# A graph-attention layer with fast matrix multiplication on one Trainium2 core: one block row of V moved ahead of P6, half of the next pair's V ahead of the first output, W's loads ahead of two of x's

## The chip, the cores and the metric

The kernel runs on one core of a Trainium2 chip. TensorE (PE in the profile) multiplies, with its weight loads shown apart as PEld; VectorE (DVE), ScalarE (ACT) and GpSimd (POOL) do the elementwise work; SyncE (SP) issues nearly all DMAs. The metric is the device time of one execution in microseconds, lower is better. Each engine takes its instructions strictly in the order in which they were written, and waits at the head of its queue for semaphores.

## What is computed

```python
output = einsum('bni,io->bno', x, w)          # V, 32 items of 256 x 512
q = einsum('bni,io->bno', x, wq)
k = einsum('bni,io->bno', x, wk)
alpha = einsum('bno,bmo->bnm', q, k)          # 256 x 256 scores of an item
alpha = maximum(alpha, 0) * (adj != 0)
alpha = softmax(alpha, axis=1)
x = layernorm(x + einsum('bnm,bmo->bno', alpha, output))   # fp32, over the last axis
```

## The kernel before

The 32 items of x go in 16 pairs. Slot 0 of the buffers belongs to the even item of work and slot 1 to the odd one: "pair 0" and "pair 1" below are the first two pairs. First G = wq·wkᵀ is formed once (`fill_g`), so that scores are (x·G)·xᵀ. T = x·G and V = x·W are then computed by a Strassen-like scheme: x is four blocks A11, A12, A21, A22, sums of them are S1 to S4, sums of G's and W's blocks are T1, T2, T3 and D4, and seven products P1, P7, P6, P5, P2, P3, P4 (each in two halves) replace eight.

Every fp32 operand X is split: `X_hi` is X cast to fp32r by ScalarE, `X_lo` is X - X_hi, computed by VectorE or GpSimd. A product is three matmuls (`add_chunk`, lines 339 to 341): hi·hi, hi·lo, lo·hi. So each product waits for splits that two other engines deliver in their own written order.

T is computed for two pairs at once (`fill_first_t`, `fill_t`), V by pair (`fill_v`, 14 halves of 6 matmuls). Only pair 0's V is computed plainly, one block row at a time: `fill_first_v(r)` for r = 0 to 3, 12 matmuls of 512 columns each. PE's order before the loop is: G; rows 0, 1, 2 of pair 0's V; `fill_first_t`; the scores of pair 0 (`fill_first_s`, 2 x 24 matmuls of 256 columns); row 3 of pair 0's V; the scores of pair 1 (`fill_s_b(0)`); the output of pair 0 (`fill_first_o`); the V of pair 1 (`fill_v(1, 1, first=True)`). Then a loop over the other groups of two pairs follows, and `fill_last_o`.

Around the scores VectorE does this, in this order: split of T's block A21 of pair 0; `mask(0, 0)` when the first 24 score matmuls are done, two row maxima; split of T's block A11 of pair 1; `mask(0, 1)`, which needs the second 24 score matmuls; split of T's block A12 of pair 1; two row maxima; splits of A22 and A21 of pair 1. `fill_scores(0, 1)` waits for pair 0's fourth T split. `fill_s_b(0)` waits for pair 1's second T split (A12) and `mask(0, 0)`, its second half for the fourth (A21) and `mask(0, 1)`.

SP issues, in order: Wq and Wk by quarters, pair 0's x (`xt`, four blocks), W (four quarters, into `xn`), pair 1's x (into `soft` and `parts`), then later pairs behind waits. GpSimd forms the sums S3, S1, S2, S4 of both pairs, splits some of them, forms T1, T3, T2, D4 of W and splits those.

## Time and profile before

| | us |
|---|---|
| median of 3 runs | 520.92 (520.74 to 521.06) |
| the profiled execution | 520.78 |
| its span in the trace | 519.0 |
| PE busy in the span | 510.6 (98%) |

The span is what the profiler saw of the program; 1.8 us lie around it. In the rows below times count from the span's start. A row of the timeline gives start, duration, engine, line, operation, output<-inputs, and, in brackets, how long the engine sat idle before it and what released it. PE's matmuls overlap, so their pace is read from the distance between starts and not from the durations. The trace shows tiles by name only: W's raw data lie in `xn`, pair 1's sums in `parts` and `adj`.

### The profile page before, as it was taken

What the parts mean: (1) busy time and instruction counts of PE and PEld (TensorE: products, weight loads), DVE (VectorE), ACT (ScalarE), POOL (GpSimd) and SP (SyncE); (2) the same over time, 40 slices, a digit from 0 to 9 for tenths busy, and PEclk for the clock granted to TensorE, in tenths of its full rate; (3) what the DMA queues carried; (4) which work ended last, traced back from release to release, by engine and by line L of the source; (5) the groups of instructions that cost most, each with busy time, mean ns of one, the idle gap of its engine ahead of it and who ended that gap; (6) DMA issues with size and microseconds to landing.
All of it is one profiled execution on the core that took longest, in us unless ns stands there. A gap on an engine that the chain in (4) does not pass through costs nothing.

```text
span 519.0 us, 9822 instructions
## 1 busy us (share of the span) xinstructions
PE 510.6 (98%) x3206; PEld 464.0 (89%) x3206; DVE 379.1 (73%) x744; ACT 330.9 (64%) x756; POOL 263.4 (51%) x199
## 2 busy tenths in 40 slices
PE   8999999999999999999999999999999999999995
PEld 7779998899989998899988999889998999889994
DVE  6997855776848677586866778577684866757586
ACT  6855756386763857649474586638676385764677
POOL 1799884339535377145651486433953537610011
PEclk9999999999999999999999999999999999999998
DMA  8412151044520626025350342405342061501426
GB/s 291 175 61 83 67 182 58 20 124 163 178 84 20 221 62 242 20 61 182 116 203 20 125 139 110 175 20 151 132 179 84 20 222 61 202 1 35 168 90 235
DMA packets 30367, 62.05 MB, mean 120 GB/s; under 512 B 2064, under 2 KB 2320, under 8 KB 30352
## 3 DMA queue, kind: packets, MB, share of 16 engines
q1 hardware_dynamic: 30064, 61.48, 34.7%
q10 hardware_dynamic: 288, 0.39, 0.2%
q8 instruction: 7, 0.11, 0.1%
q14 instruction: 8, 0.07, 0.0%
HBM read 45.09 MB, written 16.78 MB: 119 GB/s over the span
## 4 chain that ended last, share of the span: by engine, by line
PE 95%; DMA 1%; SPq 1%; DVE 1%; issue 1%; ACT 0%; POOLq 0%; POOL 0%; DVEq 0%; ACTq 0%
PE o_bank L339 12%; PE o_bank L340 12%; PE o_bank L341 12%; PE chain L339 11%; PE chain L341 11%; PE chain L340 11%; PE bank_y L339 6%; PE bank_y L340 6%; PE bank_y L341 6%; PE bank_z L341 3%; PE bank_z L340 3%; PE bank_z L339 3%; DMA xn<-in_w 1%; SPq L293 0%; SPq L289 0%
## 5 line engine op out<-in xcount | busy, mean ns | idle before, releaser
L1560 POOL TENSOR_TENSOR s_lo<-xs,s_hi 128x512 fp32r<-128x512 f32 x56 | 76.4, 1378 | 36.7 <-ACT s_hi L727 36.7
L1555 POOL TENSOR_TENSOR a_lo<-xt,a_hi 128x512 fp32r<-128x512 f32 x42 | 57.5, 1375 | 61.3 <-ACT a_hi L719 61.3
L339 PE MATMUL o_bank<-t_hi,a_hi 128*128 128x256 f32 x256 | 72.5, 283 | 0.0
L340 PE MATMUL o_bank<-t_lo,a_hi 128*128 128x256 f32 x256 | 72.4, 283 | 0.0
L341 PE MATMUL o_bank<-t_hi,a_lo 128*128 128x256 f32 x256 | 72.4, 283 | 0.0
L1565 POOL TENSOR_TENSOR rstd<-var_eps,minus_half 128x4 f32<-128x4 f32 x14 | 14.2, 1017 | 92.6 <-DVE var_eps L1202 92.6
L750 ACT COPY parts<-chain 128x256 f32<-128x256 f32 x90 | 33.2, 369 | 43.3 <-PE chain L341 42.1
L1122 DVE TENSOR_TENSOR parts<-parts,bank_y 128x512 f32<-128x512 f32 x32 | 22.0, 688 | 41.9 <-ACT parts L736 25.8
L1551 POOL TENSOR_TENSOR xs<-xt 128x512 f32<-128x512 f32 x28 | 36.8, 1325 | 27.9 <-DMA xt<-in_x_t 27.9
L339 PE MATMUL chain<-w_hi,s_hi 128*128 128x256 f32 x180 | 50.9, 283 | 0.0
L340 PE MATMUL chain<-w_lo,s_hi 128*128 128x256 f32 x180 | 50.9, 283 | 0.0
L341 PE MATMUL chain<-w_hi,s_lo 128*128 128x256 f32 x180 | 50.9, 283 | 0.0
L1188 DVE SCALAR_TENSOR_TENSOR xn<-o_bank,xn 128x512 f32<-128x512 f32 x62 | 42.4, 684 | 10.2 <-PE o_bank L341 10.1
L339 PEld LDWEIGHTS o_bank<-t_hi,a_hi 128*128 128x128 f32 x256 | 49.1, 192 | 0.4
L340 PEld LDWEIGHTS o_bank<-t_lo,a_hi 128*128 128x128 f32 x256 | 49.1, 192 | 0.4
L341 PEld LDWEIGHTS o_bank<-t_hi,a_lo 128*128 128x128 f32 x256 | 49.1, 192 | 0.0
L339 PE MATMUL o_bank<-v_hi,p_hi 128*128 128x512 f32 (+1 forms) x126 | 49.0, 389 | 0.1
L340 PE MATMUL o_bank<-v_lo,p_hi 128*128 128x512 f32 (+1 forms) x126 | 48.9, 388 | 0.0
L341 PE MATMUL o_bank<-v_hi,p_lo 128*128 128x512 f32 (+1 forms) x126 | 48.8, 387 | 0.0
L1110 DVE TENSOR_TENSOR v_lo<-parts,v_hi 128x512 fp32r<-128x512 f32 x45 | 46.8, 1052 | 0.1
L1208 DVE TENSOR_SCALAR xn<-xn,neg_mean,rstd 128x512 f32<-128x512 f32 x56 | 39.3, 723 | 10.1 <-POOL rstd L1565 10.1
L778 ACT CAST t_hi<-parts 128x512 fp32r<-128x512 f32 x24 | 14.8, 621 | 49.8 <-PE o_bank L341 49.8
(209 smaller groups left out, 1648.6 us busy)
## 6 DMA issues: line engine op xcount, KB each, us to landing
xn<-in_x SPq DMA_DIRECT2D x16, 1024.0 KB, 5.2
xt<-in_x_t SPq DMA_DIRECT2D x60, 256.0 KB, 3.1
out<-xn SPq DMA_DIRECT2D x14, 1024.0 KB, 5.3
adj<-in_adj_t SPq DMA_DIRECT2D x16, 512.0 KB, 4.8
xn<-in_wq_t SPq DMA_DIRECT2D x4, 256.0 KB, 4.0
xn<-in_w SPq DMA_DIRECT2D x4, 256.0 KB, 6.9
out<-xn SPq DMA_DIRECT2D x2, 512.0 KB, 3.1
parts<-in_wk_t SPq DMA_DIRECT2D x3, 256.0 KB, 4.5
```

Source lines behind the costliest of these rows:

```text
L339: nc.tensor.matmul(dst, a[0], b[0], start=first, stop=False, skip_group_check=shared)
L340: nc.tensor.matmul(dst, a[0], b[1], start=False, stop=False, skip_group_check=shared)
L341: return nc.tensor.matmul(dst, a[1], b[0], start=False, stop=last, skip_group_check=shared)
L750: nc.scalar.copy(parts[:, PART[product], c, 0], chain_v[:, c]).then_inc(v_copied, 1)
L778: nc.scalar.copy(t_hi[:, u], whole).then_inc(t_hi_ready, 1)
L1110: return nc.vector.tensor_tensor(dst, whole, hi.bitcast(F32), ALU.subtract)
L1122: nc.vector.tensor_tensor(part, part, bank, ALU.add).then_inc(t_summed, 1)
L1188: nc.vector.scalar_tensor_tensor(out=xn[:, slot, r], in0=row.rearrange("q j n -> q (j n)"), scalar=1.0, in1=xn[:, slot, r], op0=ALU.mult, ...
L1208: nc.vector.tensor_scalar(xn[:, slot, r], xn[:, slot, r], neg_mean[:, r:r + 1], rstd[:, r:r + 1], ALU.add, ALU.mult).then_inc(normed, 1)
L1551: nc.gpsimd.tensor_tensor(xs[:, s], a, b, op).then_inc(x_summed[slot], 1)
L1555: nc.gpsimd.tensor_tensor(a_lo[:, slot, u], xt[:, u], a_hi[:, slot, u].bitcast(F32), ALU.subtract).then_inc(a_lo_ready[slot], 1)
L1560: nc.gpsimd.tensor_tensor(s_lo[:, slot, s], xs[:, s], s_hi[:, slot, s].bitcast(F32), ALU.subtract).then_inc(s_lo_ready[slot], 1)
```

## The change

It has four parts.

1. PE: `fill_first_v(3)` moves from behind `fill_first_s` to between P7 and P6 in `fill_first_t`. It writes `o_bank[2]` now, and waits for `g_lo_ready` 3 and the first D4 half. ScalarE's and VectorE's `split_first_v(3)` move forward with it.
2. PE: the first six of the fourteen halves of pair 1's V (`open_v`) come before `fill_first_o`, the other eight (`close_v`) after it. ScalarE's copies of P1 and P6 of pair 1 move ahead of some casts and of pair 1's four exponents.
3. SP, ScalarE, VectorE: W is loaded and split between x's blocks A12 and A21. GpSimd waits for all of pair 0's x to be split before it forms the first sum.
4. Pair 0's S2 is split by GpSimd and not by VectorE. Semaphore targets follow.

```diff
-FIRST_LO = {S3: 1, S2: 2}, {S1: 1, S4: 2}
+FIRST_LO_DVE = {S3: 1}, {S3: 1, S2: 2}
+FIRST_LO_POOL = {S2: 1, S1: 2, S4: 3}, {S1: 1, S4: 2}
...
-        v0_bank = [bank_y[:, 0], o_bank[0][:], o_bank[1][:], o_bank[0][:]]
+        v0_bank = [bank_y[:, 0], o_bank[0][:], o_bank[1][:], o_bank[2][:]]
...
+            load_x0(A11)
+            load_x0(A12)
             for k in range(K):
                 sp.dma_start(w_raw[:, k], w_rows[:, k]).then_inc(w_loaded[k], 16)
+            load_x0(A21)
+            load_x0(A22)
...
                 pe.wait_ge(gt_summed, 8)
                 t_half(P7, 1, both)
+
+                fill_first_v(3)
                 pe.wait_ge(t_copied, 1)
...
                 if r == 3:
 
-                    pe.wait_ge(t_summed, 2)
+                    pe.wait_ge(g_lo_ready, 3)
+                    pe.wait_ge(gt_summed, G_SUMMED[D4, 0])
...
                 fill_scores(0, 0)
+
+                pe.wait_ge(v_lo_ready, 4)
                 pe.wait_ge(t_lo_ready, 4)
                 fill_scores(0, 1)
...
             fill_first_s()
-            fill_first_v(3)
             fill_s_b(0)
+
+            pe.wait_ge(wt_lo_ready, W_ORDER.index(D4))
+            open_v(1, 1)
             fill_first_o()
-            fill_v(1, 1, first=True)
+            close_v(1, 1, first=True)
...
-            exponent(1, 0)
-            exponent(1, 1)
-            copy_v(1, P1, 0)
-            exponent(1, 2)
-            copy_v(1, P1, 1)
-            exponent(1, 3)
             copy_v(1, P6, 0)
             copy_v(1, P6, 1)
+            for r in range(R):
+                exponent(1, r)
...
-            pool.wait_ge(qk_lo_ready, 2 * K)
+            pool.wait_ge(a_lo_ready[0], 4)
             sum_first_x(0, S3)
-
-            pool.wait_ge(w_lo_ready, K)
             sum_first_x(0, S1)
...
             sum_first_x(1, S2)
+            split_first_s(0, S2)
             split_first_s(0, S1)
```

PE's queue where P7 ends and P6 begins, before. `bank_y<-s` is P7, `chain<-s` is P6:

```order
L341 MATMUL bank_y<-s_hi,g_lo 128x512
L339 MATMUL chain<-s_hi,g_hi 128x512
L340 MATMUL chain<-s_lo,g_hi 128x512
L341 MATMUL chain<-s_hi,g_lo 128x512
...
```

PE's queue at the same place in the changed kernel (its `add_chunk` has lines 350 to 352); `o_bank2<-w` is row 3 of pair 0's V, four such groups of three:

```order
L352 MATMUL bank_y<-s_hi,g_lo 128x512
L350 MATMUL o_bank2<-w_hi,a_hi 128x512
L351 MATMUL o_bank2<-w_lo,a_hi 128x512
L352 MATMUL o_bank2<-w_hi,a_lo 128x512
...
L350 MATMUL chain<-s_hi,g_hi 128x512
L351 MATMUL chain<-s_lo,g_hi 128x512
...
```

Twelve matmuls now stand between P7 and P6. PE's queue behind the scores of pair 0, before; `o_bank2<-t` is the second half of pair 0's scores, `o_bank0<-w` row 3 of V (twelve matmuls), `o_bank1<-t` the scores of pair 1:

```order
L341 MATMUL o_bank2<-t_hi,a_lo 128x256
L339 MATMUL o_bank0<-w_hi,a_hi 128x512
L340 MATMUL o_bank0<-w_lo,a_hi 128x512
L341 MATMUL o_bank0<-w_hi,a_lo 128x512
...
L339 MATMUL o_bank1<-t_hi,a_hi 128x256
...
```

The same place in the changed kernel, and where pair 1's scores end (`chain<-w` is the first product of pair 1's V):

```order
L352 MATMUL o_bank2<-t_hi,a_lo 128x256
L350 MATMUL o_bank1<-t_hi,a_hi 128x256
L351 MATMUL o_bank1<-t_lo,a_hi 128x256
...
L352 MATMUL o_bank2<-t_hi,a_lo 128x256
L350 MATMUL chain<-w_hi,a_hi 128x256
L351 MATMUL chain<-w_lo,a_hi 128x256
...
```

Nothing stands between the two pairs' scores any more. VectorE's queue from the split of T's block A21 of pair 0 (`t_lo<-parts`) over `mask(0, 0)` (`soft<-adj,o_bank1`) and `mask(0, 1)` (`o_bank2`) to the split of A12 of pair 1 (`t_lo<-c12_b`) is, in the kernel before:

```order
L1110 TENSOR_TENSOR t_lo<-parts,t_hi 128x512
L1161 SCALAR_TENSOR_TENSOR soft<-adj,o_bank1 128x512
L1167 TENSOR_SCALAR soft,neg_max<-soft 128x256 x2
L1110 TENSOR_TENSOR t_lo<-parts,t_hi 128x512
L1161 SCALAR_TENSOR_TENSOR soft<-adj,o_bank2 128x512
L1110 TENSOR_TENSOR t_lo<-c12_b,t_hi 128x512
```

In the changed kernel these six stand in the same order (lines 1133, 1184 and 1190).

## Rows read from the trace of the kernel before

**Rows 1.** The page: busy time of each engine, share of the span.

```profile
PE 510.6 (98%) x3206; PEld 464.0 (89%) x3206; DVE 379.1 (73%) x744; ACT 330.9 (64%) x756; POOL 263.4 (51%) x199
```

**Rows 2.** Waits of PEld, whole span: engine, tile, line, releaser; total, times, longest.

```profile
PEld chain L339 <- issue: 1.6, 1, 1.6
...
PEld bank_y L339 <- DVE w_lo L1110: 0.5, 1, 0.5
```

**Rows 3.** Busy time by stretch: engines with instruction counts, PEclk, DMA share, GB/s.

```profile
0.00:60.00 60.00, 57.30 (x289) 48.90 (x290) 50.01 (x74) 39.81 (x79) 42.35 (x33) 1.00 0.41 141
60.00:500.00 440.00, 440.00 (x2824) 402.71 (x2823) 316.07 (x636) 277.42 (x650) 218.10 (x163) 1.00 0.33 112
```

**Rows 4.** The chain that ended last, 14 to 60 us: start, duration, what.

```profile
7.68 7.12 DMA xn<-in_w
...
16.33 0.69 DVE w_lo L1110
```

**Rows 5.** Timeline of PE at five places.

```profile
16.57 0.39 PE L341 MATMUL bank_y<-s_hi,t_lo 128*128 128x512 f32 x1
...
17.63 0.39 PE L341 MATMUL bank_y<-w_hi,a_lo 128*128 128x512 f32 x1
...
33.29 0.39 PE L341 MATMUL bank_y<-s_hi,g_lo 128*128 128x512 f32 x1
34.86 0.47 PE L339 MATMUL chain<-s_hi,g_hi 128*128 128x512 f32 x1 [1.18 <-issue]
...
35.40 0.40 PE L341 MATMUL chain<-s_hi,g_lo 128*128 128x512 f32 x1
...
48.61 0.28 PE L341 MATMUL o_bank<-t_hi,a_lo 128*128 128x256 f32 x1
...
49.10 0.28 PE L341 MATMUL o_bank<-t_hi,a_lo 128*128 128x256 f32 x1
...
51.61 0.28 PE L341 MATMUL o_bank<-t_hi,a_lo 128*128 128x256 f32 x1
51.73 0.40 PE L339 MATMUL o_bank<-w_hi,a_hi 128*128 128x512 f32 x1
...
54.48 0.28 PE L339 MATMUL o_bank<-t_hi,a_hi 128*128 128x256 f32 x1
...
75.77 0.40 PE L339 MATMUL bank_y<-s_hi,g_hi 128*128 128x512 f32 x1
```

**Rows 6.** Timeline of DVE around the splits that PE waits for.

```profile
29.59 1.78 DVE L1110 TENSOR_TENSOR s_lo<-xs,s_hi 128x512 fp32r<-128x512 f32 x1
...
33.00 1.76 DVE L1110 TENSOR_TENSOR g_lo<-xn,g_hi 128x512 fp32r<-128x512 f32 x1
34.68 0.68 DVE L1110 TENSOR_TENSOR v_lo<-o_bank,v_hi 128x512 fp32r<-128x512 f32 x1
...
47.51 1.19 DVE L1110 TENSOR_TENSOR t_lo<-parts,t_hi 128x512 fp32r<-128x512 f32 x1 [0.69 <-ACT t_hi L762]
...
50.44 1.22 DVE L1110 TENSOR_TENSOR t_lo<-parts,t_hi 128x512 fp32r<-128x512 f32 x1
51.93 0.69 DVE L1161 SCALAR_TENSOR_TENSOR soft<-adj,o_bank 128x512 f32<-128x512 int32 x1 [0.28 <-PE o_bank L341]
52.54 0.83 DVE L1110 TENSOR_TENSOR t_lo<-c_b,t_hi 128x512 fp32r<-128x512 f32 x1
...
55.08 0.66 DVE L1110 TENSOR_TENSOR t_lo<-parts,t_hi 128x512 fp32r<-128x512 f32 x1
```

**Rows 7.** Timeline of POOL, 49 to 75 us.

```profile
49.82 4.70 POOL L1625 TENSOR_TENSOR w_lo<-xn,w_hi 128x512 fp32r<-128x512 f32 x3
55.42 1.46 POOL L1560 TENSOR_TENSOR s_lo<-xs,s_hi 128x512 fp32r<-128x512 f32 x1 [0.90 <-ACT s_hi L727]
58.03 1.50 POOL L1560 TENSOR_TENSOR s_lo<-xs,s_hi 128x512 fp32r<-128x512 f32 x1 [1.14 <-ACT s_hi L727]
...
73.14 1.51 POOL L1560 TENSOR_TENSOR s_lo<-xs,s_hi 128x512 fp32r<-128x512 f32 x1 [0.20 <-ACT s_hi L727]
```

More of the change, by code:

```diff
@@ L291, in _, with load_x0 @@
                     sp.dma_start(wk_raw[:, k], wk_rows[:, k]).then_inc(wk_loaded[k], 16)
-            for u in range(4):
+            def load_x0(u):
                 sp.dma_start(xt[:, u], x_t[0].rearrange("q (u k n) -> q u k n", u=4, k=2)[:, u]).then_inc(
                     x0_loaded[u], 16)
+            load_x0(A11)
+            load_x0(A12)
             for k in range(K):
                 sp.dma_start(w_raw[:, k], w_rows[:, k]).then_inc(w_loaded[k], 16)
+            load_x0(A21)
+            load_x0(A22)
             for u in (A11, A21, A12, A22):
@@ L482, in fill_first_t, with v_copy_taken, open_v @@
                 t_half(P4, 1, both)
-            def fill_v(p, slot, first=False):
-                def copy_taken(n):
-                    pe.wait_ge(v_copied, COPIES * (p - 1) + n)
-                if first:
-                    pe.wait_ge(wt_lo_ready, W_ORDER.index(D4))
+            def v_copy_taken(p, n):
+                pe.wait_ge(v_copied, COPIES * (p - 1) + n)
+            def open_v(p, slot):
                 v_half(P1, 0, slot)
@@ L494, in fill_v, with close_v @@
                 v_half(P7, 0, slot)
-                copy_taken(1)
+                v_copy_taken(p, 1)
                 v_half(P6, 0, slot)
-                copy_taken(2)
+                v_copy_taken(p, 2)
                 v_half(P6, 1, slot)
                 v_half(P7, 1, slot)
-                copy_taken(3)
+            def close_v(p, slot, first=False):
+                v_copy_taken(p, 3)
                 v_half(P5, 0, slot)
-                copy_taken(4)
+                v_copy_taken(p, 4)
                 v_half(P5, 1, slot)
@@ L505, in fill_v @@
                 v_half(P2, 1, slot)
-                copy_taken(5)
+                v_copy_taken(p, 5)
                 v_half(P3, 0, slot)
-                copy_taken(6)
+                v_copy_taken(p, 6)
                 v_half(P3, 1, slot)
@@ L514, in fill_v @@
                 v_half(P4, 1, slot)
+            def fill_v(p, slot):
+                open_v(p, slot)
+                close_v(p, slot)
             def v0_parts(r, k):
@@ L633, in fill_first_o @@
             def fill_first_o():
+                pe.wait_ge(t_summed, 2)
                 pe.wait_ge(v_lo_ready, R)
@@ L1024, in _ @@
                 split_wq(k)
-            for u in range(4):
-                split_x0(u)
+            split_x0(A11)
+            split_x0(A12)
             for k in range(K):
                 split_w(k)
+            split_x0(A21)
+            split_x0(A22)
             split_g(0)
@@ L1053, in _ @@
             split_first_a(A21)
+            split_first_v(3)
             copy_first_t(P6, 0)
@@ L1075, in _ @@
                 split_p(0, r, first=True)
-            split_first_v(3)
             split_s(1, 0, S3, first=True)
@@ L1081, in _ @@
             split_a(1, 0, A11, first=True)
+            copy_v(1, P1, 0)
+            copy_v(1, P1, 1)
             split_s(1, 0, S1, first=True)
@@ L1371, in _ @@
                 split_qk(wq_lo, wq_raw, wq_hi, k, 2 * k + 1)
-            for u in range(4):
-                split_x0(u + 1, u)
+            split_x0(1, A11)
+            split_x0(2, A12)
             for k in range(K):
@@ L1378, in _ @@
                      w_hi[:, b:b + 2, k % 2]).then_inc(w_lo_ready, 1)
+            split_x0(3, A21)
+            split_x0(4, A22)
             dve.wait_ge(qk_lo_ready, 2 * K)
@@ L1407, in _ @@
             split_gt(D4)
+            split_first_v(3)
             sum_t(0, A22, 0, first=True)
@@ L1431, in _ @@
                 split_p(0, r)
-            split_first_v(3)
             mask(1, 0)
```

19 lines of the change are left out of this document (10 added, 9 removed).

## The prediction

> **What bounds the kernel now.** I read the page's busy times first: PE is busy for 98% of the span [rows 1]. The table by stretches says where the rest lies: from 60 to 500 us PE is busy in every microsecond, at a granted clock of 1.00, and in the first 60 us it is busy for 57.30 [rows 3]. All that the change touches ends before or just behind 60 us, so it can only win back pauses of PE in the prologue, and any pause that it makes anew adds to the time in full, since PE has no slack later on to take it up. Third, the waits of PE's weight loads name the pauses: one before P6, one before row 0 of pair 0's V [rows 2]. Last, PE's timeline gives their true price, as distance between starts against the undisturbed pace [rows 5]. Row 3 of V shows the pace at 512 columns: 12 starts from 51.73 to 54.48, so 2.75 us in all and 0.23 us each. At 256 columns it is 0.12 us (51.61 to 51.73).
>
> **Part 1a, row 3 ahead of P6: a gain of 1.42 us.** From the last matmul of P7 at 33.29 to the third of P6 at 35.40 lie 2.11 us for three starts, which take 0.69 undisturbed: 1.42 us are lost there [rows 5]. P6 waits for T2's rest, VectorE's `g_lo` that runs from 33.00 to 34.76 [rows 6]. PE would now spend 2.75 us on row 3 in that place, longer than the wait, so the wait is gone even if VectorE comes no earlier. It does come earlier, since it no longer splits pair 0's S2 (1.78 us at 29.59 [rows 6]). What is late next there? S2 of pair 0 comes from GpSimd now, as the seventh operation of its queue; at up to 1.8 us each from a start near 16 it is out by 29, against P6 at about 36. The new waits of row 3 are for results that VectorE writes before T3's rest, on which P7 waits already. `split_first_v(3)` is 0.68 us on VectorE, as row 2's at 34.68 [rows 6], and falls where VectorE waits for P6 anyway. I cost these at nothing.
>
> **Part 3, W ahead of two of x's blocks: a gain of 0.37 us.** Row 0 of V starts late: 16.57 to 17.63 is 1.06 us for three starts, 0.37 too long [rows 5]. It waits for W's last rest at 16.33 to 17.02, eighth in the line of splits, and that line hangs on the DMA that lands at 14.80 [rows 4]. The same eight loads come in a different order, so the eighth still lands then, but row 0 no longer needs it: the W rest is sixth, two places of about 0.6 us earlier, and ready before 16. GpSimd's first sum now comes behind all eight. That moves its queue by somewhat under a microsecond, and the extra S2 split adds up to 1.8; no wait of PE up to P4 hangs closely on it.
>
> **Part 1b, the cover that row 3 was: a loss of about 1.9 us.** Row 3 stood between the scores of pair 0 and those of pair 1. Before, `mask(0, 1)` starts at 51.93, 0.20 us behind the point N = 51.73 at which PE goes on from pair 0's scores; the split of A12 of pair 1 follows at 52.54 and ends at 53.37, so N + 1.64 [rows 6]. PE takes up pair 1's scores at 54.48 [rows 5], 1.11 us later. The 2.75 us of row 3 covered all of it. In the changed order PE asks for that split at N itself, and VectorE's order there is unchanged: first the mask, which needs the very last score matmul, then the split. PE must wait about N + 1.64 plus what it takes to start again. That is read where the second half of pair 0's scores waits: its split ends at 47.51 + 1.19 = 48.70 [rows 6], and the third matmul behind it starts at 49.10 [rows 5], 0.40 us later where two steps take 0.24. So 0.16, and 1.80 us in all. The bounds: if GpSimd doesn't block the split at all it takes 0.68 and not 0.83, which gives 1.65; if it is blocked for one whole GpSimd operation (some 1.2 us), 2.85. I take 1.9, nearer to the row than to the end, because three splits in this stretch took 1.19, 1.22 and 0.83 [rows 6]: 0.40 above 0.68 on average, where this one had 0.15.
>
> **The same blocking at two more places: 0.4 us.** Before, the pause ahead of the second half of pair 0's scores is small: 48.61 to 49.10 is 0.49 for three steps that take 0.36 undisturbed, so 0.13 us [rows 5]. It hangs on a split of 1.19 us, 0.51 of which is blocking [rows 6]. GpSimd will be at another operation by then (it is moved by some 2 us, PE and VectorE by 2.75 - 1.42 - 0.37 = 0.96), so that blocking may be anything from 0 to 1.2: the pause changes by -0.13 to +0.69. I take +0.3. The second half of pair 1's scores needs the last T split. It ended at 55.74, N + 4.01 [rows 6], and PE would ask for it 1.80 + 24 x 0.12 = 4.68 us behind N. That is 0.6 to spare, but GpSimd's three `w_lo` splits, which ended at 54.52 and left the last T split alone [rows 7], will reach about a microsecond further into this place. I take +0.1, bounds 0 and 0.6.
>
> **Part 2, half of pair 1's V ahead of the first output: nothing.** The matmuls are the same. Before, PE had no pause there [rows 3], so there is none to win. The six halves take 36 x 0.12 = 4.3 us and need copies of P1 by ScalarE between them; ScalarE's queue is arranged for this. `close_v` begins where the second half of V began before, so all that hangs on it (P5's copies, the sums) keeps its distance. The residual sums of pair 0 come 4.3 us later on VectorE, which had been waiting for P5's copies behind them. The loop's first product asks for GpSimd's split at 73.14 to 74.65; PE starts it at 75.77, 1.1 us later [rows 5, 7]. GpSimd's shift of some 2 us is mostly used up before that by its idle 0.90 and 1.14 us [rows 7], where it waits for ScalarE.
>
> **Sum.** -1.42 - 0.37 + 1.9 + 0.3 + 0.1 = +0.5 us. Against the profiled execution (520.78, span 519.0) that is 521.3; against the median of the runs shown, 520.92, it is 521.4. The lower ends of the costs give -1.79 + 1.65 - 0.13 = -0.3, so 520.6; the upper ends -1.79 + 2.85 + 0.69 + 0.6 = +2.35, so 523.3. A measurement of this kernel tells about 0.2% (1.04 us) from no change.
>
> **The rivals.** (A) The forecast: the pause moves from P6 to the scores of pair 1. For it speaks that the mask depends on PE's last score matmul and the split stands behind the mask. Time 520.6 to 521.9, chance 0.64.
>
> (B) Slower: GpSimd blocks the splits on which PE now waits. On VectorE a split from SBUF took 1.78 and 1.76 us where GpSimd is busy, the same split from PSUM 0.68 [rows 6]. From the point at which the new pauses together pass 1.79 + 1.04 = 2.8 us the kernel is measurably slower. One fully blocked split before pair 1's scores (2.85) and the +0.3 above make +1.36, so 522.3. Against it: three full blocks in a row are unlikely, 0.83 was seen at this very place. Chance 0.20. The Trainium skill ("SBUF — State Buffer", section "Who interferes with whom") says that a VectorE instruction with two SBUF inputs and a GpSimd instruction that reads SBUF exclude each other, the later one waiting for all of the first. By that rule the upper ends above, one whole GpSimd operation each, can occur, and the trace's 1.78 beside 0.68 agrees with it.
>
> (C) GpSimd's delay reaches the loop: if it comes over 1.1 us later than PE's own shift at the split of 73.14, each further 0.1 us is lost on PE. Chance 0.06, around 522.1.
>
> (D) Faster: pair 1's scores hardly wait. To show as a gain the new pauses must stay under 1.79 - 1.04 = 0.75 us, less than mask and split take together (1.44 from 51.93 to 53.37). It needs PE to be held elsewhere while VectorE goes on, or a pause in the prologue that I don't see and that the change removes. 519.1 with no wait at all; chance 0.09. That the change doesn't do what it says (P6 still waiting, for GpSimd's S2) would leave +0.5 + 1.42, 522.8; chance 0.01.
>
> **Numbers.** 521.4, as (A) has most of the chance. Range 520.4 to 522.6: it drops most of (D) and the far end of (B). Faster by over 0.2% 0.09, within 0.2% 0.65, slower 0.26.
>
> **What would show it.** Right: no idle time of PE before P6 and none before row 0 of V; a new idle time of 1.5 to 2.5 us at the first matmul of pair 1's scores, released by VectorE's `t_lo`; PE busy without a break from there to 500 us. Part by part: `w_lo`'s last split before the last `a_lo`; T2's rest ending near 32 or 33. Wrong: PE at pair 1's scores without a pause, or with pauses in the loop's first group.

## The result and the profile after

| | before | after |
|---|---|---|
| median, side by side on one chip | 521.06 us (15 runs) | 521.94 us (15 runs, 521.12 to 522.93) |
| ratio | | 1.0018, 95% interval 1.0010 to 1.0025 |
| the profiled execution | 520.78 us | 521.65 us |
| its span | 519.0 us | 519.8 us |
| PE busy | 510.6 us | 510.1 us |

The changed kernel is 0.9 us slower. A second comparison (below) gave 1.0022, just beyond 0.2%. The forecast was 521.4, with a range of 520.4 to 522.6 and "within 0.2%" as the likeliest case. The sign, the range and the case held; the sum of +0.5 us was some 0.4 us too small, and the time lies at the upper end of case (A) (520.6 to 521.9), next to the 522.1 of case (C). One of the two signs of being wrong that the prediction named came as well: a pause in the loop's first group.

The table by stretches of the changed kernel, as [rows 3] was for the one before. The columns are the stretch and its length, then busy time with instruction counts of PE, PEld, DVE, ACT and POOL, PEclk, DMA share and GB/s:

```profile
0.00:60.00 60.00, 56.82 (x291) 48.41 (x292) 48.66 (x71) 39.46 (x77) 43.57 (x34) 1.00 0.41 141
60.00:500.00 440.00, 439.20 (x2815) 401.69 (x2814) 318.27 (x638) 277.02 (x648) 221.29 (x163) 1.00 0.33 112
```

PE was busy 57.30 us of the first 60 and for all of the other 440. Now it is 0.48 less in the first stretch, and the second stretch is no longer whole: 0.80 us are missing there. The waits of PEld in the changed kernel say where (engine, tile, line, releaser; total, times, longest):

```profile
PEld o_bank L350 <- DVE t_lo L1133: 2.1, 2, 1.6
...
PEld bank_y L350 <- POOL s_lo L1585: 1.0, 1, 1.0
```

The two waits of [rows 2] are gone. In their place stand two for VectorE's T splits and one of the loop's first product (`bank_y`) for GpSimd's split `s_lo`. PE's timeline of the changed kernel gives their price, as [rows 5] did:

```profile
15.79 0.39 PE L352 MATMUL bank_y<-s_hi,t_lo 128*128 128x512 f32 x1
16.02 0.39 PE L350 MATMUL bank_y<-w_hi,a_hi 128*128 128x512 f32 x1
...
34.83 0.39 PE L352 MATMUL o_bank<-w_hi,a_lo 128*128 128x512 f32 x1
35.06 0.39 PE L350 MATMUL chain<-s_hi,g_hi 128*128 128x512 f32 x1
...
51.86 0.28 PE L352 MATMUL o_bank<-t_hi,a_lo 128*128 128x256 f32 x1
53.56 0.39 PE L350 MATMUL o_bank<-t_hi,a_hi 128*128 128x256 f32 x1 [1.43 <-DVE t_lo L1133]
...
56.41 0.28 PE L352 MATMUL o_bank<-t_hi,a_lo 128*128 128x256 f32 x1
57.00 0.36 PE L350 MATMUL o_bank<-t_hi,a_hi 128*128 128x256 f32 x1 [0.31 <-issue]
...
75.37 0.28 PE L352 MATMUL bank_y<-w_hi,a_lo 128*128 128x256 f32 x1
76.45 0.50 PE L350 MATMUL bank_y<-s_hi,g_hi 128*128 128x512 f32 x1 [0.80 <-POOL s_lo L1585]
76.79 0.39 PE L351 MATMUL bank_y<-s_lo,g_hi 128*128 128x512 f32 x1
```

Row 0 of V (16.02) and P6 (35.06) follow at the undisturbed 0.23 us. The rest is counted as in the prediction, three steps less their undisturbed time (0.23 us at 512 columns, 0.12 at 256), since the first steps behind a pause are slower too (76.45 to 76.79 is 0.34). All pauses of PE between 14 and 85 us, in both profiled executions:

| place | before | after |
|---|---|---|
| row 0 of pair 0's V | 0.38 | 0 |
| P6 | 1.43 | 0 |
| pair 0's scores, first half | 0 | 0.28 |
| pair 0's scores, second half | 0.13 | 0 |
| pair 1's scores, first half | 0 | 1.68 |
| pair 1's scores, second half | 0 | 0.54 |
| the loop's first product | 0 | 1.08 |
| sum | 1.94 | 3.58 |

That is 1.64 us more; the span grew by 0.8. The other 0.8 lies ahead of all these places: the last product of G began at 14.08 us in the profile before and at 13.30 in the one after. The account closes: in each of the fourteen profiled executions of this text the span is this start, plus the pauses, plus what a fallen clock costs (two executions, below), plus 502.8 to 503.0 us. The start itself lay between 13.21 and 14.21 in them, in kernels with the same code up to there as well. So a span alone cannot be compared to better than about 1 us here, and every experiment below is read by its pauses and by its ratio over many runs.

VectorE in the changed kernel, around the new waits (start, duration, what):

```profile
52.17 0.69 DVE L1184 SCALAR_TENSOR_TENSOR soft<-adj,o_bank 128x512 f32<-128x512 int32 x1 [0.35 <-PE o_bank L352]
52.78 0.73 DVE L1133 TENSOR_TENSOR t_lo<-c_b,t_hi 128x512 fp32r<-128x512 f32 x1
...
55.21 1.69 DVE L1133 TENSOR_TENSOR t_lo<-parts,t_hi 128x512 fp32r<-128x512 f32 x1
56.83 5.82 DVE L1201 SCALAR_TENSOR_TENSOR p_lo<-soft,inv_sum,p_hi 128x256 fp32r<-128x256 f32 x4
```

The mask starts 0.19 us behind the point (51.98) at which PE is through with pair 0's scores, the split ends at 53.51, and PE goes on at 53.56: the pause of 1.68 is mask plus split, as forecast. The last T split at 55.21 takes 1.69 us where it took 0.66 before [rows 6], and PE's second half waits for it. Behind it the four `p_lo` splits take 5.82 us together. In the kernel before they took less than half of that:

```profile
55.87 2.49 DVE L1178 SCALAR_TENSOR_TENSOR p_lo<-soft,inv_sum,p_hi 128x256 fp32r<-128x256 f32 x4
```

GpSimd in the changed kernel, over the same time and up to the loop:

```profile
51.23 5.12 POOL L1649 TENSOR_TENSOR w_lo<-xn,w_hi 128x512 fp32r<-128x512 f32 x3
56.32 3.18 POOL L1585 TENSOR_TENSOR s_lo<-xs,s_hi 128x512 fp32r<-128x512 f32 x2
...
68.78 1.29 POOL L1576 TENSOR_TENSOR xs<-xt 128x512 f32<-128x512 f32 x1
73.42 1.29 POOL L1576 TENSOR_TENSOR xs<-xt 128x512 f32<-128x512 f32 x1 [3.35 <-DMA xt<-in_x_t]
74.67 1.73 POOL L1585 TENSOR_TENSOR s_lo<-xs,s_hi 128x512 fp32r<-128x512 f32 x1
```

The same from the kernel before:

```profile
68.27 1.29 POOL L1551 TENSOR_TENSOR xs<-xt 128x512 f32<-128x512 f32 x1
71.65 1.29 POOL L1551 TENSOR_TENSOR xs<-xt 128x512 f32<-128x512 f32 x1 [2.08 <-DMA xt<-in_x_t]
```

The three `w_lo` reach to 56.35 now (54.52 before [rows 7]), past the start of the last T split (55.21). The sum that leads to the loop's first product starts 1.77 us later in the trace, 0.51 of it GpSimd's own delay (68.27 to 68.78) and 1.26 waiting for a DMA. That DMA is the fourth block of x of a pair that the loop works on. SP's queue in the changed kernel (start of issue, its duration):

```profile
68.89 0.33 SPq L242 DMA_DIRECT2D xt<-in_x_t  x1
69.27 0.43 SPq L265 DMA_DIRECT2D xn<-in_x  x1
```

And in the kernel before:

```profile
68.39 0.33 SPq L238 DMA_DIRECT2D xt<-in_x_t  x1
68.77 1.32 SPq L261 DMA_DIRECT2D xn<-in_x  x1
```

From issue to GpSimd's start on it the block took 3.26 us before (68.39 to 71.65) and 4.53 after (68.89 to 73.42). The 1 MB load issued right behind it occupied SP's queue for 1.32 us before and for 0.43 after.

### The profile page after: what moved, and what is told of

It is laid out like the page before. It is cut to its first block, busy times and chain, and to the rows that moved or that the text cites. A ratio compares the mean times of both kernels' runs of the same rounds, so it can differ in the third digit from the quotient of the medians.

```text
span 519.8 us, 9804 instructions
## 1 busy us (share of the span) xinstructions
PE 510.1 (98%) x3206; PEld 463.3 (89%) x3206; DVE 380.7 (73%) x743; ACT 331.0 (64%) x756; POOL 267.8 (52%) x200
## 3 DMA queue, kind: packets, MB, share of 16 engines
HBM read 45.09 MB, written 16.78 MB: 119 GB/s over the span
## 4 chain that ended last, share of the span: by engine, by line
PE 83%; POOL 9%; DMA 2%; DVE 2%; issue 1%; SPq 0%; ACT 0%; POOLq 0%; DVEq 0%; ACTq 0%
PE o_bank L350 10%; PE o_bank L351 10%; PE o_bank L352 10%; PE chain L352 10%; PE chain L351 10%; PE chain L350 10%; PE bank_y L350 5%; PE bank_y L351 5%; PE bank_y L352 5%; PE bank_z L352 3%; PE bank_z L351 3%; PE bank_z L350 3%; DMA xt<-in_x_t 1%; POOL xs L1576 1%; POOL s_lo L1555 1%; POOL w_lo L1649 1%
## 5 line engine op out<-in xcount | busy, mean ns | idle before, releaser
L1133 DVE TENSOR_TENSOR v_lo<-parts,v_hi 128x512 fp32r<-128x512 f32 x45 | 48.2, 1081 | 0.8 <-ACT v_hi L811 0.7
L759 ACT COPY parts<-chain 128x512 f32<-128x512 f32 x42 | 24.6, 587 | 34.0 <-PE chain L352 33.5
```

Source lines behind the costliest of these rows:

```text
L759: nc.scalar.copy(parts[:, PART[product], c], chain[:, c]).then_inc(t_copied, 1)
L1133: return nc.vector.tensor_tensor(dst, whole, hi.bitcast(F32), ALU.subtract)
```

## The experiments

Twelve runs, two of them of the kernels as they are. Pauses are counted as above. Medians of different comparisons are not set against each other; the ratio to the kernel before, measured on the same chip, is.

**The changed kernel again.**

> The changed kernel once more, nothing edited. My theory: its new pauses of PE are four, each with its cause: about 0.3 us before pair 0's scores, 1.7 before pair 1's scores (mask and split behind PE's last score matmul), 0.5 before their second half (a split blocked by GpSimd), and 1.1 before the loop's first product (GpSimd's split of S3). They should all be there again, the last within 0.5 us, and the time about 0.9 us over the kernel before. Rival: the 0.9 us between the two kernels is the start of the program (matmuls of G began 0.8 us apart in the two profiles) and has nothing to do with those pauses: then they come and go while the difference stays, or the difference falls below 0.3 us.

Measured: 522.22 us against 520.95, ratio 1.0022 (1.0008 to 1.0035). Pauses 3.36 in all: 0.80 at the second half of pair 0's scores, 1.71 at pair 1's first half, 0.85 at the loop. What follows: the long pause at pair 1's scores and the one at the loop are there again, but the two small ones move with the phase between GpSimd and VectorE. Here GpSimd's `w_lo` x3 took 4.68 us and not 5.12, was through at 55.78, and the second half of pair 1's scores had no pause, while pair 0's second half had one.

**Part 1 undone** (row 3 of V back between the two pairs' scores; the rest stays).

```diff
-        v0_bank = [bank_y[:, 0], o_bank[0][:], o_bank[1][:], o_bank[2][:]]
+        v0_bank = [bank_y[:, 0], o_bank[0][:], o_bank[1][:], o_bank[0][:]]
...
                 t_half(P7, 1, both)
-
-                fill_first_v(3)
...
             fill_first_s()
+            fill_first_v(3)
             fill_s_b(0)
```

> Part 1 undone alone: row 3 of pair 0's V is behind pair 0's scores again, everything else as changed. Both theories: no pause before P6, since T2's rest ends near 32.2 and PE asks at 33; none before row 0; none before pair 1's scores, row 3 covers them. Theory A (the loop's first product is bound by GpSimd's chain: split of A22, DMA of the next pair's A22, sum S1, split of S3, ready at 76.4 in the changed kernel whatever PE does): PE arrives at the loop near 74.0 and waits 2.4 us, so nothing of the 1.8 us is kept and the time is 521.4 to 522.0. Theory B (the loop's pause follows PE, as GpSimd comes earlier when PE does): the pause there stays near 1 us or less and the time is 519.3 to 520.3.

Measured: 520.81 us against 520.95, ratio 1.0000 (0.9991 to 1.0009). The pauses at the scores are gone (0.04 left), and so is the one before P6. New ones stand inside T's products, 0.58 and 0.50, and the loop's is 1.37. Neither theory had this: A had the loop's pause at 2.4 and the time at 521.4 or more, B at 1 or less and 520.3 at most, and neither had a pause in T. PE and ScalarE of this kernel:

```profile
34.92 0.39 PE L352 MATMUL chain<-s_hi,g_lo 128*128 128x512 f32 x1
35.60 0.50 PE L350 MATMUL chain<-s_hi,g_hi 128*128 128x512 f32 x1 [0.29 <-ACT parts L764]
```

```profile
33.41 0.62 ACT L1019 CAST s_hi<-adj 128x512 fp32r<-128x512 f32 x1 [1.08 <-POOL adj L1547]
...
34.97 1.06 ACT L764 COPY parts<-chain 128x512 f32<-128x512 f32 x2
```

ScalarE stood waiting for GpSimd's late sum until 33.41; the copy that frees PE's bank is queued behind that sum's cast and two others, and came at 34.97. What follows: part 1 turns 520.8 into 521.9, so with the other parts in place it costs about 1 us (1.0018 and 1.0022 against 1.0000). And the shift of GpSimd has a price of its own that part 1 hides: without row 3 in front of P6, PE comes to P6 some 2.7 us earlier (32.40) and meets ScalarE's late copies.

**Part 1 alone** (on the kernel before).

```diff
 # on the kernel before
                 t_half(P7, 1, both)
+
+                fill_first_v(3)
...
             fill_first_s()
-            fill_first_v(3)
             fill_s_b(0)
```

> The kernel before with part 1 alone: row 3 of pair 0's V between P7 and P6, with its splits. Theory: it wins the 1.4 us before P6 and pays them back before pair 1's scores (1.6 to 1.9 us there, plus 0 to 0.5 at the second halves where GpSimd blocks a split); GpSimd is not later than before, so no pause at the loop. Time 0 to 0.8 us over the kernel before. Rival (part 1 is a gain by itself and the loss of the changed kernel comes from GpSimd alone): the time is 0.8 us or more under the kernel before.

Measured: 521.73 us against 520.97, ratio 1.0015 (1.0006 to 1.0024). Pauses: P6 none; 0.56 at pair 0's second half; 1.70 at pair 1's first half; none at its second half and none at the loop. So part 1 by itself trades 1.43 for 1.70 + 0.43. The pause at row 0 was 1.12 in this execution (0.38 before, 0.20 when the kernel before was profiled again):

```profile
17.26 0.50 PE L339 MATMUL bank_y<-w_hi,a_hi 128*128 128x512 f32 x1 [0.83 <-DVE w_lo L1115]
```

Part 1 does not touch that. W's last rest ended at 17.22, 17.02 and 16.78 in the three profiles of kernels that load W behind all of x, while the last product of G began at 13.55, 14.08 and 14.03: the earlier PE is through with G, the longer it stands there. What follows: the whole step "P6's pause moves to pair 1's scores" stands, and the loop's pause does not come from part 1.

**Part 3 alone** (on the kernel before: W's loads and splits between x's blocks, GpSimd's first sum behind all of x).

```diff
 # on the kernel before
-            pool.wait_ge(qk_lo_ready, 2 * K)
+            pool.wait_ge(a_lo_ready[0], 4)
             sum_first_x(0, S3)
-
-            pool.wait_ge(w_lo_ready, K)
             sum_first_x(0, S1)
```

> The kernel before with part 3 alone: W loaded and split ahead of x's A21 and A22, GpSimd starting behind all of them. Theory: no pause before row 0 of V (0.37 us won); VectorE is about 0.9 us earlier, so T2's rest ends near 33.9 and the pause before P6 falls from 1.4 to about 0.9; GpSimd is at most 0.5 us later, with no pause at the loop (1.1 us to spare before, less the 0.9 won). Time 0.6 to 0.9 us under the kernel before. Rival (GpSimd's later start reaches the loop): a pause of over 0.3 us there, and the time within 0.3 us of the kernel before.

Measured: 524.60 us (524.26 to 526.33, 5 runs) against 520.97, ratio 1.0069 (1.0055 to 1.0083). A clear miss: a gain of 0.6 to 0.9 us was expected and the kernel is 3.6 us slower. The pause of row 0 is gone and P6's is 1.40. What I did not see is behind the scores. VectorE, PE and the stretches of this kernel:

```profile
56.41 5.79 DVE L1185 SCALAR_TENSOR_TENSOR p_lo<-soft,inv_sum,p_hi 128x256 fp32r<-128x256 f32 x4
62.13 0.68 DVE L1117 TENSOR_TENSOR v_lo<-o_bank,v_hi 128x512 fp32r<-128x512 f32 x1
```

```profile
59.68 0.28 PE L346 MATMUL o_bank<-t_hi,a_lo 128*128 128x256 f32 x1
62.86 0.80 PE L344 MATMUL o_bank<-v_hi,p_hi 128*128 128x512 f32 x1 [2.90 <-DVE v_lo L1117]
63.46 0.63 PE L345 MATMUL o_bank<-v_lo,p_hi 128*128 128x512 f32 x1
63.88 0.63 PE L346 MATMUL o_bank<-v_hi,p_lo 128*128 128x512 f32 x1
```

```profile
64.20:68.40 4.20, 4.20 (x11) 3.24 (x11) 1.87 (x11) 1.09 (x4) 4.20 (x5) 0.50 0.37 136
```

GpSimd comes later, so all four `p_lo` splits fall beside its own operations: 5.79 us where they took 2.49 in the kernel before. Row 3's `v_lo` is queued behind them, and the first output needs it: PE stands for 3.06 us (59.80 to 62.86). Behind the pause the granted clock is 0.50 up to 68.40, the 1.2 GHz level, and PE's steps are 0.42 us where they take 0.23 otherwise. The profiled execution is the longest of the five, 1.5 us above the next. Its mean granted clock was 0.992, that of the other four 0.994 or 0.995, where the kernel before had 0.997 or more beside it; so the clock fell in all five, and less in the four. The loop's fourth block is the other finding. SP's queue and GpSimd of this kernel:

```profile
68.36 0.33 SPq L238 DMA_DIRECT2D xt<-in_x_t  x1
68.74 0.43 SPq L261 DMA_DIRECT2D xn<-in_x  x1
```

```profile
72.93 1.29 POOL L1560 TENSOR_TENSOR xs<-xt 128x512 f32<-128x512 f32 x1 [3.39 <-DMA xt<-in_x_t]
```

The short issue of `xn` and the long way of the block before it (4.57 us) are here with part 3 and nothing else. In part 1 alone the issue lasts 1.22 us and the block takes 3.14. What follows for the changed kernel: parts 1 and 2 are not only trades. Row 3's early split takes `v_lo` out from behind `p_lo`, and the six halves of pair 1's V stand between the scores and the output that needs `p_lo`.

**Part 2 undone** (pair 1's V whole again behind the first output).

```diff
-            pe.wait_ge(wt_lo_ready, W_ORDER.index(D4))
-            open_v(1, 1)
             fill_first_o()
+            pe.wait_ge(wt_lo_ready, W_ORDER.index(D4))
+            open_v(1, 1)
             close_v(1, 1, first=True)
```

ScalarE's copies of P1 and P6 and the four exponents go back to their places too.

> The changed kernel with part 2 alone undone: the second half of pair 1's row 0 of V stands behind the first output again, and ScalarE's casts stand as in the kernel before. In the profile of the changed kernel VectorE's four p_lo splits last from 56.83 to 62.65 (each about 1.5 us, blocked by GpSimd's own split), and the mask of the first output's row 1 stands behind them. Theory 1 (the half row in front is what covers these splits): without it TensorE comes to the first output's row 1 near 61.3 and waits there 1.5 to 2.2 us for the mask, perhaps with a granted clock of 0.50 behind it as in the kernel with part 3 alone; the wait of 1.07 us at the loop's first product goes, since TensorE comes there later. Time 0.8 to 1.5 us above the changed kernel's 521.9, more if the clock falls. Theory 2 (part 2 is worth nothing, as the prediction had it): no wait of over 0.4 us near the first output, the loop's wait stays about 1 us, and the time is within 0.3 us of 521.9.

Measured: 522.89 us against 520.78, ratio 1.0037 (1.0027 to 1.0047), so 0.0019 or 1.0 us above the changed kernel. PE of this kernel:

```profile
61.27 0.39 PE L352 MATMUL o_bank<-v_hi,p_lo 128*128 128x512 f32 x1
63.39 0.50 PE L350 MATMUL o_bank<-v_hi,p_hi 128*128 128x512 f32 x1 [1.73 <-DVE soft L1186]
```

A pause of 2.01 before the output's row 1, released by the mask behind `p_lo`, and none at the loop, which PE reaches at 77.70. The granted clock stays 1.00 behind this one. 2.01 - 1.08 = 0.93 against 1.0 measured. What follows: theory 1 holds. Part 2, which the prediction put at nothing, is worth about 1 us once parts 3 and 4 have moved GpSimd.

**Part 4 undone** (pair 0's S2 split by VectorE again).

```diff
-FIRST_LO_DVE = {S3: 1}, {S3: 1, S2: 2}
+FIRST_LO_DVE = {S3: 1, S2: 2}, {S3: 1, S2: 2}
...
             sum_first_x(1, S2)
-            split_first_s(0, S2)
             split_first_s(0, S1)
```

> The changed kernel with part 4 undone: VectorE splits pair 0's S2 again, GpSimd has one split less. Theory: T2's rest ends near 34, still before PE has done row 3 (35.2 to 35.9), so no pause before P6. GpSimd's whole queue comes 1.2 to 1.7 us earlier: the last T split of pair 1 is blocked less or not at all (that pause of 0.5 us falls to 0 to 0.3), the pause before the loop's first product is gone or under 0.3, the pause before pair 1's scores stays at 1.5 to 2.2. Time 0.8 to 1.5 us under the changed kernel. Rival (GpSimd's place in its queue does not matter, ScalarE's casts set its pace from 60 us on): the pause at the loop stays within 0.3 us and so does the time.

Measured: 521.24 us against 520.83, ratio 1.0007 (0.9999 to 1.0016). Pauses 0.38 and 1.71 at the scores, none at the second half of pair 1's, 0.81 at the loop. The expectation missed in part: the loop's pause was to be under 0.3 and the time 0.8 to 1.5 us under the changed kernel; by the ratios it is 0.6 under, and the intervals overlap. VectorE and GpSimd of this kernel:

```profile
55.54 0.66 DVE L1133 TENSOR_TENSOR t_lo<-parts,t_hi 128x512 fp32r<-128x512 f32 x1
```

```profile
50.31 4.67 POOL L1649 TENSOR_TENSOR w_lo<-xn,w_hi 128x512 fp32r<-128x512 f32 x3
```

`w_lo` ends at 54.98, before the last T split starts at 55.54, and the split takes 0.66. In the changed kernel `w_lo` ended at 56.35 and the split took 1.69. What follows: the 0.54 us pause in the changed kernel goes with the split blocked beside GpSimd's `w_lo`. It stands (0.54 to 0.56) in six of the seven profiles of kernels that have part 4 and no row 3 between the scores, and in neither of the two with part 4 undone. So part 4's extra operation in GpSimd's queue makes it likely, and the repeat of the changed kernel shows that it does not always bring it.

**The loop's block without its neighbour** (SP issues the 1 MB load of `xn` only when the fourth block has landed).

```diff
                     sp.wait_ge(wt_lo_ready, 4)
+                    sp.wait_ge(xt_loaded[A22], 32)
```

> The changed kernel with one more wait on SP: the 1 MB load of pair 1's rows of x, which is issued 0.4 us behind the fourth block of pair 3, waits until that block has landed. Theory: the 4.1 to 4.6 us that the block took to land in the changed kernels are shared bandwidth with that 1 MB load; alone it lands in about 3.1 us, GpSimd's sum S1 and split of S3 come 1.2 us earlier, the 0.7 to 1.1 us pause before the loop's first product is gone and the time is 0.7 to 1.1 us under the changed kernel. Rival (the block is slow for another reason): it still takes over 4 us, and the time is within 0.3 us of the changed kernel.

Measured: 520.69 us against 520.83, ratio 0.9994 (0.9986 to 1.0003). GpSimd and SP of this kernel:

```profile
72.29 1.29 POOL L1577 TENSOR_TENSOR xs<-xt 128x512 f32<-128x512 f32 x1 [2.06 <-DMA xt<-in_x_t]
```

```profile
69.05 0.33 SPq L242 DMA_DIRECT2D xt<-in_x_t  x1
```

By the ratios this is 1.2 us or more under the changed kernel, where 0.7 to 1.1 was expected. The block takes 3.24 us from issue to use; there is no pause at the loop, and the pauses at the scores are 0.29, 1.91 and 0.56. What follows: the loop's pause hangs on this block, and in this kernel the block is slow only with other loads issued right behind it. SP's wait holds back the 1 MB load and all that SP issues after it, so that it is the 1 MB load alone is likely but not shown. Nor is it enough by itself: the kernel before issues the same load as closely behind the block and is not slowed.

**The kernel before again, profiled.**

> The kernel before once more, for its profile. My theory of the start: the first matmuls of G begin and keep pace as the DMAs and the clock of that execution allow, so G's last part begins anywhere between 13.3 and 14.2 us in every kernel, this one too (14.08 in the first profile). The pauses before row 0 of V (0.37) and before P6 (1.42) should be there again within 0.3 us, none before pair 1's scores and none at the loop. The fourth block of pair 3 landed 3.3 us behind its issue in the first profile, and 4.1 to 4.6 in five profiles of changed kernels: if 3.3 comes again, the change makes it longer; if over 4, it was one execution's luck.

Measured: 520.57 us. Pauses 0.20, 1.41, 0.13, the same three places. SP of this run:

```profile
68.16 0.33 SPq L238 DMA_DIRECT2D xt<-in_x_t  x1
68.54 1.46 SPq L261 DMA_DIRECT2D xn<-in_x  x1
```

The long issue of `xn` (1.46) and the short way of the block before it (3.25 us to GpSimd's 71.41) are there again. What follows: the difference belongs to the kernels and not to one execution. With the kernels of part 1 alone and part 3 alone it goes with part 3: without it (three profiles) the issue lasts 1.22 to 1.46 us and the block takes 3.1 to 3.3, with it 0.43 and 4.2 to 4.6, in every profile in which SP doesn't wait in between. Why a different order of the first loads does this 60 us later stays open.

**S3 of the loop's first odd item ahead of S1's sum** (its split on GpSimd no longer waits for the fourth block; ScalarE's cast for it moves ahead of P5's copies).

```diff
             sum_x(1, 1, S3)
+            split_s(1, 1, S3)
             sum_x(1, 1, S1)
-            split_s(1, 1, S3)
```

> The changed kernel with S3 of pair 3 (slot 1) split by GpSimd right behind its sum and ahead of the sum S1 that waits for a DMA, and ScalarE's cast of it moved ahead of the copies of P5. My theory: the split is ready near 72 instead of 76.4, the pause of 1.07 us before the loop's first product is gone (another may show that was hidden behind it: v_lo of pair 1, ready near 75.9, on which P1 right behind it waits), and the time is 0.6 to 1.1 us under the changed kernel, about that of the kernel before. Rival (that pause is an accident of one profile, or something else is late by the same amount): within 0.3 us of the changed kernel.

Measured: 520.62 us against 520.95, ratio 0.9990 (0.9981 to 1.0000). No pause at the loop. GpSimd of this kernel:

```profile
70.93 1.30 POOL L1585 TENSOR_TENSOR s_lo<-xs,s_hi 128x512 fp32r<-128x512 f32 x1 [0.73 <-ACT s_hi L750]
```

The split now fills GpSimd's idle time and is out 3.4 us before PE asks for it (75.61). The scores' pauses are as they were (0.20, 1.68, 0.54). What follows: a second, independent way of taking the loop's pause away gives 1.5 us by the ratios (1.0018 to 0.9990), for 1.16 us of pauses less.

**P1's two halves of pair 1's V as the cover between the scores.**

```diff
             fill_first_s()
+            v_half(P1, 0, 1)
+            v_half(P1, 1, 1)
             fill_s_b(0)
```

> The changed kernel with both halves of P1 of pair 1's V (12 matmuls of 256 columns, 1.44 us) put between the scores of pair 0 and those of pair 1, as a cover; the rest of open_v stays. The pause before pair 1's scores should fall from 1.7 to about 0.2 us under my theory (mask and split take their time whatever PE does meanwhile); if instead the split only starts when something else is done, it stays above 1. Theory A (loop's first product bound by GpSimd's chain): the 1.44 us come back there, the pause at the loop grows from 1.1 to about 2.5, the time is within 0.4 us of the changed kernel. Theory B: the time is 1.0 to 1.5 us under the changed kernel.

Measured: 521.97 us (521.52 to 524.46) against 520.95, ratio 1.0027 (1.0014 to 1.0040). The pause before pair 1's scores shrinks from 1.68 to 0.24, and most of that 1.44 comes back at the loop, whose pause grows by 1.12:

```profile
74.56 0.28 PE L352 MATMUL bank_y<-w_hi,a_lo 128*128 128x256 f32 x1
76.75 0.50 PE L350 MATMUL bank_y<-s_hi,g_hi 128*128 128x512 f32 x1 [1.92 <-POOL s_lo L1586]
```

```profile
77.80:81.00 3.20, 3.20 (x9) 2.52 (x8) 1.33 (x2) 2.07 (x4) 3.03 (x3) 0.50 0.27 91
```

The pause is 2.20 there, and behind it the granted clock is 0.50 for 3.2 us, the lower level, which costs half of that, 1.6 us. The eleven times fall into two groups, six at 521.52 to 521.97 and five at 523.25 to 524.46, and the profiled execution (523.60) is of the second. The mean granted clock of each execution agrees: 0.993 to 0.996 in the slower group, 0.996 to 0.999 in the faster. So the groups are most likely executions with and without the fall of the clock; only one of them has a trace. What follows: as long as GpSimd's split is late, little of the time won at the scores is kept, and some executions lose more than was won.

**Both of these together.**

> P1's two halves as a cover between the two pairs' scores, together with the early split of S3 of pair 3. Theory: the cover gives its 1.44 us this time, since the loop's first product no longer waits for GpSimd: pause before pair 1's scores about 0.2, before their second half about 0.5, at the loop under 0.3, PE's granted clock 1.00 throughout. Time 1.2 to 1.5 us under the kernel with the early split alone, about 519.2. Rival (another result is late by the same amount, v_lo of pair 1 or the copies of the loop's first product): the 1.44 us come back as a pause between 74 and 90 us and the time stays near 520.6.

Measured: 519.66 us against 520.83 (29 runs), ratio 0.9976 (0.9968 to 0.9985). Pauses 0.27 and 0.55 at pair 1's scores and one of 0.29 at 80.44. What follows: with the loop's split in time the cover keeps part of its gain: by the ratios 0.7 us below the early S3 alone (0.9976 against 0.9990), where on the changed kernel it gave nothing. The expectation was 1.2 to 1.5, and by the pauses of the two profiles it is 1.3. The profiled execution was the fastest of the twelve (519.25), so its pauses are not those of the median. The kernel is 0.2% faster than the one before.

**All together, with part 4 undone and SP's wait.**

> The changed kernel with P1's two halves as the cover between the scores, S3 of pair 3 split early, S2 of pair 0 back on VectorE and the 1 MB load held until pair 3's fourth block is there. Theory: against the kernel with cover and early split alone, the pause of 0.5 us before the second half of pair 1's scores goes, since GpSimd is through its w_lo splits then, and a pause of up to 0.5 before the second half of pair 0's scores may come in its place (phase of GpSimd); nothing at the loop. Time within 0.5 us of 519.6, so 519.1 to 519.8. Rival: P6 waits for T2's rest again, as VectorE does one more split (34 against PE at 35.2 or later); then a pause shows before P6 and the time is over 520.

Measured: 519.15 us (518.88 to 520.44) against 520.97, ratio 0.9969 (0.9959 to 0.9979), the best version. The stretches of this kernel:

```profile
0.00:60.00 60.00, 57.87 (x303) 49.91 (x304) 48.95 (x74) 39.98 (x79) 41.72 (x33) 1.00 0.41 141
60.00:500.00 440.00, 440.00 (x2824) 402.75 (x2823) 316.92 (x643) 278.86 (x654) 220.66 (x163) 1.00 0.32 113
```

PE is busy 57.87 of the first 60 us and without a gap from there on. Two pauses are left, 0.17 and 0.28.

The pauses in one place (us). "Scores 0" is both halves of pair 0's scores; "scores 1" is pair 1's, by half; "T" is inside T's products; "clock" is what a granted clock of 0.50 cost beside the pauses:

| kernel | V row 0 | P6 | T | scores 0 | scores 1, first | scores 1, second | output | loop | sum | ratio |
|---|---|---|---|---|---|---|---|---|---|---|
| before | 0.38 | 1.43 | 0 | 0.13 | 0 | 0 | 0 | 0 | 1.94 | 1 |
| after | 0 | 0 | 0 | 0.28 | 1.68 | 0.54 | 0 | 1.08 | 3.58 | 1.0018 |
| part 1 alone | 1.12 | 0 | 0 | 0.56 | 1.70 | 0 | 0 | 0 | 3.38 | 1.0015 |
| part 3 alone | 0 | 1.40 | 0 | 0 | 0 | 0 | 3.1 + clock | 0 | 4.5 + clock | 1.0069 |
| part 1 undone | 0 | 0 | 1.08 | 0.04 | 0 | 0 | 0 | 1.37 | 2.49 | 1.0000 |
| part 2 undone | 0 | 0 | 0 | 0.15 | 1.91 | 0.54 | 2.01 | 0 | 4.61 | 1.0037 |
| part 4 undone | 0 | 0 | 0 | 0.38 | 1.71 | 0 | 0 | 0.81 | 2.90 | 1.0007 |
| best | 0 | 0 | 0 | 0.17 | 0.28 | 0 | 0 | 0 | 0.45 | 0.9969 |

## Why the prediction was right, point by point

**What bounds the kernel: right.** The forecast was that a new pause adds to the time in full. In each of the fourteen profiled executions the span less its start, its pauses and the clock's cost is 502.8 to 503.0 us, while the pauses go from 0.45 (best version) to 4.61 (part 2 undone).

**Part 1a, P6: right.** 1.42 were to be won, 1.43 were. T2's rest ended at 32.19 (the forecast was 32 or 33) and P6 started at 35.06. The claim that the new waits cost nothing holds. That the S2 split on GpSimd would not hold P6 holds too, but the sentence that GpSimd's shift touches nothing "up to P4" holds only thanks to part 1: with it undone, ScalarE's queue stood behind GpSimd's sums and T lost 1.08 us.

**Part 3, row 0: right in mechanism, most likely too small.** 0.37 was forecast, and the pause of 0.38 in that profile is gone. But the 0.37 was read from one execution in which G ended late. W's last rest came at about 17.0 whenever G ended, so the pause takes up an early start: start and pause together are 14.46, 14.23 and 14.67 us in the three profiles without part 3. In the eleven with it no pause follows, and the start is 13.21 to 14.21, in the mean 13.61. So part 3 seems worth some 0.8 us here, an estimate from three profiles against eleven.

**Part 1b, the cover: right in mechanism, 0.2 too dear.** 1.9 was taken, with a reading of 1.80 and bounds of 1.65 and 2.85. It measured 1.68 to 1.71 in five profiles with nothing between the two pairs' scores and 1.91 in two, where the split took 0.96. In the profile of the changed kernel the split was nearly free of blocking (0.73), and PE took the work up 0.05 us behind its end.

**"The same blocking at two more places, 0.4": the size was off at the second.** Pair 0's second half: +0.3 taken. It was -0.13 in the profile of the changed kernel, where the pause is gone, and +0.67 in the repeat, both at the ends of the range of -0.13 to +0.69. The 0.28 of that profile stand at pair 0's first half, a place that the prediction did not name; the split that PE waits for there is queued behind two others that took 3.46 us together. That the sum of the two (+0.15) is near +0.3 is luck. Pair 1's second half: +0.1 taken, 0.54 measured, inside 0 to 0.6. The step that failed is "GpSimd's three `w_lo` splits will reach about a microsecond further into this place". Their end came 1.83 us later in the trace and, against the point N at which PE leaves pair 0's scores, 1.6 us (54.52 - 51.73 = 2.79 before, 56.35 - 51.98 = 4.37 after), far enough to hold up the last T split (1.69 us). Part 4 undone took this pause away. In the repeat of the changed kernel it was absent as well: there `w_lo` ended at 55.78 and the split began at 56.35.

**Part 2, "nothing": wrong, twice.** First, it is worth about 1 us. I asked whether PE had a pause there before, and it had none; I did not ask whether the other parts would make one. GpSimd's later queue doubled `p_lo` (2.49 to 5.82 us), and the first output would have waited 2.0 us for the mask behind it, had the six halves of pair 1's V not stood in front (part 2 undone shows it). Second, the same paragraph holds the error that brought the loop's pause.

**Rival (C), the loop: it happened, with a chance of 0.06.** Its time, 522.1, is nearer to the median of 521.94 than the forecast of 521.4 is, and a pause in the loop's first group was one of the prediction's signs of being wrong. The spare 1.1 us was read correctly, and so was GpSimd's own shift: against PE's it came about 0.8 us later at 68.78, within the spare. The step that failed is that only GpSimd's queue was followed. The split hangs on a sum, the sum on a block of x, the block's issue on GpSimd's last use of the buffer, and that block took 1.26 us longer. With 0.22 more for a blocked split and 0.24 less in front of it, 0.8 + 1.26 - 0.02 = 2.04 us stand against 1.12 of spare: 0.9, and 0.1 for slower first steps, against 1.08 measured. The two edits that reach this wait from different sides, SP's wait and the early S3, each removed it, at 0.9994 and 0.9990. The 1.26 us come with part 3 (as the experiments show), and nothing in the profile of before shows that they would. What could be read there is how the 1.1 us of spare are made up: a DMA stands in the middle of the chain, and a change that reorders DMAs was weighed only at the place where it reorders them.

**Sum.** -1.43 - 0.38 + 1.68 + 0.15 + 0.54 + 1.08 = +1.64 by the pauses of the two profiles, +0.9 by the medians. Between the two profiled executions the difference of 0.8 is the start of G's last product (14.08 and 13.30). The forecast of +0.5 left out 1.08 at the loop and 0.44 at pair 1's second half, and was near partly by luck: an early start, which the kernel before loses at row 0, seems to stay with the changed one (part 3, above), and that gain was not in the sum either. How much of it the medians hold is an estimate, since fourteen executions have a trace and the start moves by 1 us between them. The start alone shows no difference: its mean was 13.61 us in the eleven profiles with part 3 and 13.89 in the three without. A slip in the chances: "P6 still waiting" (0.01, 522.8) is slower by more than 0.2% and was counted as within it.

**(B), blocking:** it made a part of the loss (0.54), not the full block before pair 1's scores by which (B) was defined. The Trainium skill ("SBUF — State Buffer", section "Who interferes with whom") says that a VectorE instruction with two SBUF inputs contends with a GpSimd instruction that reads SBUF. The trace agrees with it for that last T split: 1.69 beside GpSimd's `w_lo` against 0.66 where GpSimd was idle as it began.

## What to carry to other kernels

When an edit delays one engine's queue, follow every chain that starts in that queue up to the first instruction of the critical engine that uses it, the transfers that wait for a buffer included, and compare the delay with the spare of that chain; a spare of 1 us is not a cover. An independent stretch of the critical engine's work can cover one late result only once: moving it moves the wait, and whether that pays is decided by how long the two waits are. Where two parts of a change touch the same engine, read each beside the others: what one part makes late can be what another part hides.

## What the runs showed of the hardware

- A VectorE split of 128x512 from SBUF took 0.66 us where GpSimd was idle as it began and up to 1.69 to 1.78 beside GpSimd's elementwise work; four `p_lo` of 128x256 took 2.49 us in the kernel before and 5.82 in the changed one, where GpSimd was at work beside all four.
- Pauses of PE of 2.20 and 3.06 us were followed by a granted clock of 0.50 for 3.2 and 5.6 us; pauses of 1.08 to 2.01 us in other profiles were followed by 1.00. In the kernel with 2.20 the times fall into two groups 1.3 us apart, and the mean granted clock of the executions is lower in the slower one (0.993 to 0.996 against 0.996 to 0.999).
- A 256 KB load at about 69 us took 3.1 to 3.3 us to its user in the three profiles without part 3 and 4.2 to 4.6 in those with it, unless the 1 MB load behind it and what follows it were held back (3.24). The issue of that 1 MB load lasted 1.22, 1.32 and 1.46 us without part 3 and 0.43 with it. Part 3 touches DMAs that are issued 60 us earlier; how it reaches this place is open.
- The start of the program, up to G's last product, took 13.21 to 14.21 us in fourteen executions. That is more than the effect studied here.
